# Gathers of two tiles issued as two each, in a DLRM tower kernel

## The chip, the cores and the metric

The kernel runs on one core of a Trainium2 chip. The metric is the device time of an execution in microseconds (us). A core has TensorE (PE in the profile) for matmuls and transposes, VectorE (DVE), ScalarE (ACT), GpSimd (POOL), which here issues the gathers, and SyncE (SP), which issues the plain loads. The engines run side by side and wait for each other through semaphores. Sixteen DMA engines move the data that POOL and SP ask for.

## The reference

A batch of 2048 samples has 32 fields. For each field a table of 1000, 1250 or 12500 rows of 256 floats is looked up with the sample's id. The 32 looked-up rows of a sample are multiplied pairwise, and three dense layers follow:

```
e = stack([tbl_f[ids[:, f]] for f in range(32)], axis=1)      # 2048 x 32 x 256
z = einsum('bnd,bmd->bnm', e, e)[:, iu, ju]                    # the 496 pairs i < j
h = concatenate([z, dense_ctx], axis=1)                        # 496 + 16 = 512 features
h = maximum(h @ W_top1 + b_top1, 0)                            # 512 x 512
h = maximum(h @ W_top2 + b_top2, 0)                            # 512 x 256
y = h @ W_top3                                                 # 256 x 1
```

All is float32.

## The kernel before

The batch is worked in 16 tiles of 128 samples, one sample to a partition. Six of the 32 fields have small tables and are looked up on PE, by matmuls of one-hot columns with a table held on the chip (`look_up`, line 338; VectorE makes the columns, line 674). The other 26 fields are gathered: POOL issues one indirect DMA per field and tile, which fetches for each of the 128 partitions the table row whose number stands in `row_ids` (line 295).

Two fields make a unit, so a tile has 13 units (tile 0 has some more, for 29 gathers); all units of all tiles stand in one list, `UNITS`, which POOL goes through in order. Gathered rows land in `rows`, which has nine places, one unit each. Before unit n is gathered, POOL waits until PE has transposed unit n − 9 (`turn_done`, line 293). Each place has a semaphore, `gathered`, which a gather raises by 16; `n_gathered` says what count PE has to see before it transposes unit n.

PE goes through the tiles in order. For one tile it transposes 13 units into four PSUM banks (`turn`, line 322), from which ScalarE (line 483) and VectorE (line 609) copy them to `turned`; the gram then multiplies the fields of each sample with each other (`gram`, line 358) in eight portions of 64 matmul records, and between the portions stand the lookups of a following tile. Four of the next tile's units are transposed early, after portions 3 to 6, the other nine after the last portion, in `turn_all`. In `turn_all`, too, the features of the tile before are turned, and layer 1 of that tile follows (line 407). ScalarE copies its result out with the bias (line 550), and layer 2 (line 420) runs after portion 0 of the gram. VectorE finishes the tile's output (lines 655 and 657). The last tile has a gram form of its own (line 377) and no lookups.

SP issues the loads in one queue: the row numbers of tile 0, ids and small tables, then the row numbers of tiles 1 to 15 (line 263), more ids, each behind the one-hot that frees its place, the other tables and the weights.

Of the kernel before, what the change touches and what calls it, by code (L numbers as in the profile page):

```python
# [7 lines left out]
FIELDS = 32  # L8
D = 256
P = 128  # L10
# [11 lines left out]
SMALL = len(SMALL_FIELDS)  # L22
SLOTS = SMALL_FIELDS + [f for f in range(FIELDS) if f not in SMALL_FIELDS]
TILES = BATCH // P


def pair_order():

    upper = np.zeros((FIELDS, FIELDS), np.int64)
    rows, cols = np.triu_indices(FIELDS, k=1)  # L30
    upper[rows, cols] = upper[cols, rows] = np.arange(PAIRS)
    upper = upper[np.ix_(SLOTS, SLOTS)]
    order = [upper[i, (i + k) % FIELDS] for i in range(FIELDS) for k in range(1, HALF)]
    order += [upper[i, i + HALF] for i in range(HALF)]
    order += list(range(PAIRS, PAIRS + CONTEXT))
    return np.array(order)


def dlrm_tower(nc, dense_ctx, ids, small_ids, tables, w1, b1, w2, b2, w3, out):
    fp32 = mybir.dt.float32  # L40
    fp32r = mybir.dt.float32r
    int32 = mybir.dt.int32
# [19 lines left out]
    UNITS = [(0, unit) for unit in PAIRED + ODD_PAIRED]  # L62
    BEGIN = [0, len(UNITS)]
# [4 lines left out]
    PLACES = 9  # L68
# [29 lines left out]
    for step in range(-1, TILES):  # L98
        FIRST[step] = len(LOOKUPS)
        n = step + 1  # L100
# [10 lines left out]
    with ctx:  # L111
        def sbuf(name, shape, dt=fp32):
            return ctx.enter_context(nc.sbuf_tensor(name, shape, dt))
# [4 lines left out]
        def sem(name):  # L118
            return ctx.enter_context(nc.semaphore(name))

        row_ids = sbuf("row_ids", [P, TILES, FIELDS], int32)
        ids_across = sbuf("ids_across", [P, IDS_RING, 2 * P], int32)
        row_numbers = sbuf("row_numbers", [SP, SUB], int32)

# [6 lines left out]
        rows = sbuf("rows", [P, PLACES, 2, D])  # L131
# [37 lines left out]
        diagonal = products[:, :].rearrange("p (i k) -> p i k", k=ZROW + 1)  # L169

        row_ids_in = [sem(f"row_ids_in{i}") for i in range(2)]
        ids_across_in = [sem(f"ids_across_in{i}") for i in range(IDS_RING)]
        dense_in = sem("dense_in")
        weights_in = sem("weights_in")
        table_in = [sem(f"table_in{i}") for i in range(SMALL)]
        gathered = [sem(f"gathered{i}") for i in range(PLACES)]
# [49 lines left out]

        def n_gathered(n):

            return 16 * sum(len(UNITS[m][1]) for m in range(n % PLACES, n + 1, PLACES))

        def n_ids(n):

# [4 lines left out]
        @block.sync  # L237
        def _(sp):
            def load_ids(n):
                f, t, tiles = LOOKUPS[n]  # L240
                if n >= IDS_RING:
                    sp.wait_ge(one_hot_made, n - IDS_RING + 1)
                sp.dma_start(ids_across[:, n % IDS_RING, 0:tiles * P],
                             small_ids[f, t * P:(t + tiles) * P].partition_broadcast(P),
                             ).then_inc(ids_across_in[n % IDS_RING], 16)

            def load_table(i):
                table = tables[i].rearrange("(p r) d -> p r d", r=SUB)
                sp.dma_start(landed[0:SP_WIDE, i, :, 1, :], table[0:SP_WIDE, :, :]).then_inc(table_in[i], 16)
                sp.dma_start(landed[SP_WIDE:SP, i, :, 1, :], table[SP_WIDE:SP, :, :]).then_inc(table_in[i], 16)  # L250

            def load_dense(t):
                if t > 0:
                    sp.wait_ge(ft_done, t)
                sp.dma_start(features[:, PAIRS:FEATURES], dense_ctx[t * P:(t + 1) * P, :]).then_inc(dense_in, 16)

            sp.dma_start(row_ids[:, 0, :], ids[:, 0, :]).then_inc(row_ids_in[0], 16)
            load_ids(0)
            load_table(0)
            load_ids(1)  # L260
            load_ids(2)
            load_table(1)
            sp.dma_start(row_ids[:, 1:TILES, :], ids[:, 1:TILES, :]).then_inc(row_ids_in[1], 16)
            load_ids(3)
            load_ids(4)
            for i in range(2, SMALL):
                load_table(i)
            load_dense(0)
            sp.dma_start(w2_sb[:, :, :], w2.rearrange("(k p) n -> p k n", p=P)).then_inc(weights_in, 16)
            sp.dma_start(w3_sb[:, :], w3.rearrange("n a -> (a n)").partition_broadcast(P)).then_inc(weights_in, 16)  # L270
            sp.dma_start(b1_sb[:, :], b1).then_inc(weights_in, 16)
            sp.dma_start(b2_sb[:, :], b2.partition_broadcast(P)).then_inc(weights_in, 16)
            for c in range(KC):
                sp.dma_start(w1_sb[:, c, :], w1[c * P:(c + 1) * P, :]).then_inc(weights_in, 16)
            load_ids(5)
            for t in range(TILES):
                if t + 2 in FIRST:
                    for n in range(FIRST[t + 1], FIRST[t + 2]):
                        load_ids(n)
                if t + 1 < TILES:  # L280
                    load_dense(t + 1)
            sp.wait_ge(y_kept, 1)
            sp.dma_start(out.rearrange("(t p) a -> t (p a)", p=P), y_rows).then_inc(y_out, 16)
            sp.wait_ge(y_out, 16)

        @block.gpsimd
        def _(pool):
            def gather(n):
                t, unit = UNITS[n]
                if n == 0 or n == BEGIN[1]:  # L290
                    pool.wait_ge(row_ids_in[t], 16)
                if n >= PLACES:
                    pool.wait_ge(turn_done, n - PLACES + 1)
                for j, f in enumerate(unit):
                    pool.indirect_dma_start(  # L295
                        out=rows[:, n % PLACES, j, :], out_offset=None, in_=tables[f],
                        in_offset=bass.IndirectOffsetOnAxis(ap=row_ids[:, t, f:f + 1], axis=0),
                    ).then_inc(gathered[n % PLACES], 16)

            pool.memset(ident[:, :], 0.0).then_inc(ident_zero, 1)  # L300
            pool.wait_ge(ident_zero, 1)
            pool.affine_select(out=ident[:, :], in_=ident[:, :], compare_op=ALU.not_equal, fill=1.0,
                               base=0, pattern=[[-1, P]], channel_multiplier=1).then_inc(ident_ready, 1)
            pool.iota(row_numbers[:, :], pattern=[[1, SUB]], base=0,
                      channel_multiplier=SUB).then_inc(row_numbers_ready, 1)
            for n in range(len(UNITS)):
                gather(n)

        @block.tensor
        def _(pe):  # L310
            def turn(n):
                _, unit = UNITS[n]
                pe.wait_ge(gathered[n % PLACES], n_gathered(n))
                if n >= RING:
                    if by_act(n - RING):
                        pe.wait_ge(act_kept, n_act_kept(n - RING))
                    else:
                        pe.wait_ge(dve_kept, n_dve_kept(n - RING))
                for c in range(CHUNKS):
                    for j in range(len(unit)):  # L320
                        at = (c * len(unit) + j) * P
                        last = pe.transpose(turn_ps[n % RING][:, at:at + P],  # L322
                                            rows[:, n % PLACES, j, c * P:(c + 1) * P], ident[:, :])
                last.then_inc(turn_done, 1)

            def look_up(n, first, end):

                f, _, tiles = LOOKUPS[n]
                width = tiles * P
                if first == 0:  # L330
                    pe.wait_ge(one_hot_made, n + 1)
                    if n < SMALL:
                        pe.wait_ge(low_parts, (f + 1) * STEPS)
                    if n > 0:
                        pe.wait_ge(look_kept, n)
                for k in range(first, end):
                    c, r, part = k // (2 * SUB), k // 2 % SUB, k % 2
                    last = pe.matmul(look_ps[:, c * width:(c + 1) * width],  # L338
                                     small[:, f, r, part, c * P:(c + 1) * P], one_hot[n % 2][:, r, 0:width],
                                     start=(r == 0 and part == 0), stop=(r == SUB - 1 and part == 1))  # L340
                if end == PRODUCTS:
                    last.then_inc(looked_up, 1)
# [394 lines left out]
```

## Time and profile before

| what | value |
|---|---|
| time, median of 2 runs | 564.79 us (564.66 to 564.92) |
| span of the profiled execution | 890.7 us (no other time of it is given) |
| PE busy | 601.0 us, 67% |
| PE weight loads busy | 524.1 us, 59% |
| VectorE busy | 225.9 us, 25% |
| ScalarE busy | 204.6 us, 23% |
| POOL busy | 398.0 us, 45%, of which 397.2 us are the 419 gathers |
| DMA | 70.97 MB, mean 80 GB/s |

The profiled execution is much longer than the timed ones, so its shares are not those of a timed run. "Issue" in it is time in which an engine waited for nothing that the profile shows, and "remote" a releaser that it could not find. Durations of POOL's gathers are those of the issuing instruction, not of the data's way.

### The profile page before, as it was taken

The page shows a single profiled execution, that of the slowest core. Times are in us where ns is not written, and L with a number is a line of the kernel's source. Part 1 is how long each engine was busy: PE and PEld are TensorE (multiplying, and loading weights), DVE is VectorE, ACT ScalarE, POOL GpSimd, SP SyncE. Part 2 cuts the span into 40 slices and gives each one's busy share as a digit, 9 for nine tenths or more (in the row PEclk, how much of TensorE's full clock was granted, in tenths as well). Part 3 has the DMA queues.
Part 4 walks back from the last instruction along what each step waited for, and adds up shares of the span by engine and source line. Part 5 has one row for each costly group of instructions (what it writes and reads, how often), then busy time and mean ns, then how long its engine had stood idle before and what let it go on. Part 6 is the DMA issues. An engine that isn't in the chain of part 4 may idle for free.

```text
span 890.7 us, 24184 instructions
## 1 busy us (share of the span) xinstructions
PE 601.0 (67%) x11019; PEld 524.1 (59%) x11019; DVE 225.9 (25%) x578; ACT 204.6 (23%) x369; POOL 398.0 (45%) x426
## 2 busy tenths in 40 slices
PE   3557668486684867748577584875848668486687
PEld 2456557375572756737467474765737657375586
DVE  3444313123130231402223032231312313123122
ACT  4252303103030030401313022130210303103042
POOL 7563625526255361543715347262462625526220
PEclk9688969698796987969789697896969969698799
DMA  9962312313122141321313224131231312313110
GB/s 220 243 204 68 99 42 77 94 44 102 43 78 83 50 107 38 83 73 56 108 37 87 63 57 118 32 96 49 70 105 39 101 41 76 88 41 90 43 38 2
DMA packets 37459, 70.97 MB, mean 80 GB/s; under 512 B 10382, under 2 KB 23438, under 8 KB 37358
## 3 DMA queue, kind: packets, MB, share of 16 engines
q0 software_dynamic: 20112, 54.95, 22.1%
q1 hardware_dynamic: 17246, 14.48, 7.0%
q8 instruction: 87, 1.43, 0.7%
q14 instruction: 14, 0.11, 0.0%
HBM read 69.39 MB, written 0.01 MB: 78 GB/s over the span
## 4 chain that ended last, share of the span: by engine, by line
PE 42%; another core or an unknown queue 30%; issue 13%; ACT 12%; DMA 1%; DVE 1%; POOL 1%; ACTq 0%; DVEq 0%
PE look_ps L338 18%; PE quad_ps L358 12%; PE top_ps L420 6%; ACT turned L501 4%; ACT turned L483 3%; PE turn_ps L322 3%; PE quad_ps L322 2%; ACT area L550 2%; ACT ahead L490 1%; DMA rows<-in_tbl,row_ids 1%; PE quad_ps L377 1%; POOL rows L295 1%; PE top_ps L407 1%; ACT products L506 0%
## 5 line engine op out<-in xcount | busy, mean ns | idle before, releaser
L295 POOL DMA_INDIRECT rows<-in_tbl,row_ids x419 | 397.2, 948 | 458.1 <-PE turn_ps L322 184.1
L338 PE MATMUL look_ps<-one_hot,small 125*128 125x256 f32 (+1 forms) x1536 | 251.9, 303 | 104.7 <-issue 92.8
L338 PEld LDWEIGHTS look_ps<-one_hot,small 125*128 125x128 f32 x1536 | 214.0, 202 | 116.6 <-issue 112.3
L358 PE MATMUL quad_ps<-turned 128*32 128x31 f32 x7680 | 140.0, 204 | 121.8 <-issue 121.5
L358 PEld LDWEIGHTS quad_ps<-turned 128*32 128x32 f32 x7680 | 108.8, 115 | 166.9 <-issue 153.3
L674 DVE TENSOR_SCALAR one_hot<-ids_across,sub_row 125x256 fp32r<-125x256 int32 (+1 forms) x384 | 112.0, 364 | 145.8 <-PE look_ps L338 126.6
L322 PE MATMUL turn_ps<-ident,rows 128*128 128x128 f32 x424 | 64.5, 282 | 28.5 <-issue 14.7
L655 DVE TENSOR_TENSOR top_ps<-top_ps,b_sb 128x256 f32<-128x256 f32 x15 | 6.5, 433 | 299.8 <-PE top_ps L420 299.8
L490 ACT ACTIVATE ahead<-look_ps 128x512 f32<-128x512 f32 (+1 forms) x48 | 28.3, 590 | 232.5 <-PE look_ps L338 219.1
L407 PE MATMUL top_ps<-area,w_sb 128*128 128x128 f32 x488 | 61.9, 276 | 19.5 <-issue 18.8
L550 ACT ACTIVATE area<-top_ps,b_sb 128x128 f32<-128x128 f32 x61 | 17.5, 368 | 227.5 <-remote 225.2
L407 PEld LDWEIGHTS top_ps<-area,w_sb 128*128 128x128 f32 x488 | 57.8, 192 | 18.1 <-issue 17.2
L322 PEld LDWEIGHTS turn_ps<-ident,rows 128*128 128x128 f32 x424 | 48.2, 143 | 31.8 <-issue 28.2
L483 ACT ACTIVATE turned<-turn_ps 128x512 f32<-128x512 f32 x57 | 35.0, 631 | 114.2 <-PE quad_ps L358 76.2
L322 PE MATMUL quad_ps<-ident,rows 128*128 128x128 f32 x414 | 60.1, 279 | 0.8 <-DMA rows<-in_tbl,row_ids 0.8
L483 ACT ACTIVATE turned<-quad_ps 128x512 f32<-128x512 f32 x55 | 33.9, 631 | 90.6 <-PE quad_ps L358 70.8
L420 PE MATMUL top_ps<-w_sb,area 128*128 128x256 f32 x120 | 49.4, 585 | 4.1 <-ACT area L550 4.1
L618 DVE STREAM_TRANSPOSE products<-quad_ps 128x992 f32<-128x992 f32 x15 | 18.3, 1217 | 127.7 <-PE quad_ps L358 127.7
L322 PEld LDWEIGHTS quad_ps<-ident,rows 128*128 128x128 f32 x414 | 46.5, 142 | 2.9 <-DMA rows<-in_tbl,row_ids 1.2
L501 ACT ACTIVATE turned<-ahead 128x768 f32<-128x768 f32 x31 | 45.0, 1552 | 0.0
L420 PEld LDWEIGHTS top_ps<-w_sb,area 128*128 128x128 f32 x120 | 35.6, 311 | 13.9 <-ACT area L550 6.1
L609 DVE COPY turned<-quad_ps 128x512 f32<-128x512 f32 (+1 forms) x49 | 33.0, 681 | 34.1 <-PE quad_ps L322 14.6
(50 smaller groups left out, 169.9 us busy)
## 6 DMA issues: line engine op xcount, KB each, us to landing
rows<-in_tbl,row_ids POOLq DMA_INDIRECT x419
ids_across<-in_small_ids SPq DMA_DIRECT2D x45, 128.0 KB
landed<-in_tbl SPq DMA_DIRECT2D x6, 896.0 KB
w_sb<-in_W_top SPq DMA_DIRECT2D x4, 256.0 KB
landed<-in_tbl SPq DMA_DIRECT2D x6, 104.0 KB
w_sb<-in_W_top SPq DMA_DIRECT2D x1, 512.0 KB
area<-in_dense_ctx SPq DMA_DIRECT2D x16, 8.0 KB
row_ids<-in_ids SPq DMA_DIRECT2D x1, 240.0 KB
```

What stands on the lines that cost most here:

```text
L295: pool.indirect_dma_start(out=rows[:, n % PLACES, j, :], out_offset=None, in_=tables[f], in_offset=bass.IndirectOffsetOnAxis(ap=row_ids[:, ...
L322: last = pe.transpose(turn_ps[n % RING][:, at:at + P], rows[:, n % PLACES, j, c * P:(c + 1) * P], ident[:, :])
L338: last = pe.matmul(look_ps[:, c * width:(c + 1) * width], small[:, f, r, part, c * P:(c + 1) * P], one_hot[n % 2][:, r, 0:width], start=(r ...
L358: last = pe.matmul(gram_ps[q * FIELDS:(q + 1) * FIELDS, g // BANK_GROUPS, at:at + COLS], turned[:, c, s, :], turned[:, c, s, 0:COLS], star ...
L407: last = pe.matmul(bank[:, m * P:(m + 1) * P], w1_sb[:, c, m * P:(m + 1) * P], features_t[:, c, :], start=(c == 0), stop=(c == KC - 1))
L420: last = pe.matmul((last_h2 if t == TILES - 1 else top_ps)[:, 0:HIDDEN2], hidden1[:, c, :], w2_sb[:, c, :], start=(c == 0), stop=(c == M1 ...
L483: act.activation(turned[:, :, :, f:f + len(unit)], turn_ps[n % RING][:, 0:CHUNKS * len(unit) * P].rearrange("p (c f s) -> p c s f", c=CHUN ...
L490: act.activation(ahead[:, f, :, 0:tiles * P], look_ps[:, 0:CHUNKS * tiles * P].rearrange("p (c s) -> p c s", c=CHUNKS), ACT.Copy).then_inc ...
L501: act.activation(turned[:, :, :, fs].rearrange("p c s f -> p f c s"), ahead[:, fs, :, half * P:(half + 1) * P], ACT.Copy).then_inc(placed, 1)
L550: act.activation(hidden1[:, m, :], bank[:, m * P:(m + 1) * P], ACT.Relu, bias=b1_sb[:, m:m + 1]).then_inc(h1_kept, 1)
L609: dve.tensor_copy(turned[:, :, :, f:f + len(unit)], turn_ps[n % RING][:, 0:CHUNKS * len(unit) * P].rearrange("p (c f s) -> p c s f", c=CHU ...
L674: last = dve.tensor_scalar(one_hot[n % 2][:, r, 0:width], ids_across[0:SP, n % IDS_RING, 0:width], sub_row[:, r:r + 1], None, ALU.is_equal)
```

## The change

In tile 4 a gather of 128 rows becomes one of rows 0 to 63 and one of rows 64 to 127; in tile 8, one of rows 0 to 123 and one of rows 124 to 127. Both of a pair raise the semaphore of the unit's place by 16, and the count that PE waits for is doubled for units of these tiles. The row numbers of the second part come from a new array, `row_ids_tail` (64 partitions, 2 × 26 numbers), which the host fills and SP loads once, behind the row numbers of tiles 1 to 15; POOL waits for it ahead of tile 4.

```diff
+SPLIT_AT = {4: 64, 8: 124}
+SPLIT_TILES = sorted(SPLIT_AT)
...
+        row_ids_tail = sbuf("row_ids_tail", [P // 2, len(SPLIT_TILES), FIELDS - SMALL], int32)
...
-            return 16 * sum(len(UNITS[m][1]) for m in range(n % PLACES, n + 1, PLACES))
+            return 16 * sum(len(UNITS[m][1]) * (2 if UNITS[m][0] in SPLIT_AT else 1)
+                            for m in range(n % PLACES, n + 1, PLACES))
...
             sp.dma_start(row_ids[:, 1:TILES, :], ids[:, 1:TILES, :]).then_inc(row_ids_in[1], 16)
+            sp.dma_start(row_ids_tail[:, :, :], tail_ids).then_inc(row_ids_tail_in, 16)
...
+                if t == SPLIT_TILES[0] and n == BEGIN[t]:
+                    pool.wait_ge(row_ids_tail_in, 16)
+                at = SPLIT_AT.get(t, P)
                 for j, f in enumerate(unit):
                     pool.indirect_dma_start(
-                        out=rows[:, n % PLACES, j, :], out_offset=None, in_=tables[f],
-                        in_offset=bass.IndirectOffsetOnAxis(ap=row_ids[:, t, f:f + 1], axis=0),
+                        out=rows[0:at, n % PLACES, j, :], out_offset=None, in_=tables[f],
+                        in_offset=bass.IndirectOffsetOnAxis(ap=row_ids[0:at, t, f:f + 1], axis=0),
                     ).then_inc(gathered[n % PLACES], 16)
+                    if at < P:
+                        tail = row_ids_tail[0:P - at, SPLIT_TILES.index(t), f - SMALL:f - SMALL + 1]
+                        pool.indirect_dma_start(
+                            out=rows[at:P, n % PLACES, j, :], out_offset=None, in_=tables[f],
+                            in_offset=bass.IndirectOffsetOnAxis(ap=tail, axis=0),
+                        ).then_inc(gathered[n % PLACES], 16)
```

## Rows read from the trace of the kernel before

**Rows 1.** The page: its head, busy time by engine, DMA engines' busy tenths in 40 slices.
```profile
span 890.7 us, 24184 instructions
...
PE 601.0 (67%) x11019; PEld 524.1 (59%) x11019; DVE 225.9 (25%) x578; ACT 204.6 (23%) x369; POOL 398.0 (45%) x426
...
DMA  9962312313122141321313224131231312313110
```

**Rows 2.** POOL's gathers: busy us, mean ns, idle before; durations minimum/median/maximum; waits by releaser.
```profile
L295 POOL DMA_INDIRECT rows<-in_tbl,row_ids x419 | 397.2, 948 | 458.1 <-PE turn_ps L322 184.1 <-PE quad_ps L322 164.5 <-issue 101.8
...
L295 POOL DMA_INDIRECT rows<-in_tbl,row_ids x419: 940/946/1098, 2.7 to 855.9; - x140
...
  issue: 101.8, 333
```

**Rows 3.** Timeline of POOL in one tile: start, duration, instruction, idle before, releaser.
```profile
351.74 0.94 POOL L295 DMA_INDIRECT rows<-in_tbl,row_ids  x1 [15.15 <-PE turn_ps L322]
...
369.02 0.94 POOL L295 DMA_INDIRECT rows<-in_tbl,row_ids  x1 [3.12 <-PE turn_ps L322]
...
390.25 0.95 POOL L295 DMA_INDIRECT rows<-in_tbl,row_ids  x1 [0.30 <-issue]
```

**Rows 4.** Timeline of PE and ACT in the same tile.
```profile
341.08 3.40 PE L420 MATMUL top_ps<-w_sb,area 128*128 128x256 f32 x8 [0.27 <-ACT area L550]
344.13 1.66 PE L338 MATMUL look_ps<-one_hot,small 125*128 125x256 f32 x11
345.72 0.76 PE L358 MATMUL quad_ps<-turned 128*32 128x31 f32 x64
...
352.71 0.59 PE L358 MATMUL quad_ps<-turned 128*32 128x31 f32 x42
...
354.80 0.66 PE L322 MATMUL turn_ps<-ident,rows 128*128 128x128 f32 x4
...
375.80 0.83 PE L407 MATMUL top_ps<-area,w_sb 128*128 128x128 f32 x6
...
380.39 0.28 PE L338 MATMUL look_ps<-one_hot,small 125*128 125x256 f32 x1 [0.42 <-issue]
...
394.56 1.14 ACT L550 ACTIVATE area<-top_ps,b_sb 128x128 f32<-128x128 f32 x4 [16.39 <-remote]
395.75 0.79 PE L420 MATMUL top_ps<-w_sb,area 128*128 128x256 f32 x1 [0.27 <-ACT area L550]
```

**Rows 5.** Timeline of PE and ACT in the last tile, the same step.
```profile
863.80 3.74 PE L407 MATMUL top_ps<-area,w_sb 128*128 128x128 f32 x32
...
867.58 1.14 ACT L550 ACTIVATE area<-top_ps,b_sb 128x128 f32<-128x128 f32 x4 [0.95 <-PE top_ps L407]
868.77 1.99 PE L420 MATMUL top_ps<-w_sb,area 128*128 128x256 f32 x8 [0.15 <-ACT area L550]
```

**Rows 6.** Two windows: length, busy (count) by engine; then granted clock, DMA share, GB/s.
```profile
341.08:344.10 3.02, 3.02 (x8) 2.46 (x8) 0.00 (x0) 0.00 (x0) 0.00 (x0) 0.52 0.02 5
868.77:870.70 1.93, 1.93 (x9) 1.44 (x9) 0.00 (x0) 0.00 (x0) 0.00 (x0) 1.00 0.00 0
```

**Rows 7.** Timeline of POOL: the first and the last gather.
```profile
2.71 1.10 POOL L295 DMA_INDIRECT rows<-in_tbl,row_ids  x1 [1.15 <-DMA row_ids<-in_ids]
...
855.87 0.95 POOL L295 DMA_INDIRECT rows<-in_tbl,row_ids  x1 [0.31 <-issue]
```

**Rows 8.** Timeline of POOL: its first wait for a place.
```profile
37.57 0.95 POOL L295 DMA_INDIRECT rows<-in_tbl,row_ids  x1 [5.00 <-remote]
```

**Rows 9.** The gathers' DMA queue (packets, MB, share of 16 engines); the iota on POOL.
```profile
q0 software_dynamic: 20112, 54.95, 22.1%
...
L304 POOL IOTA row_numbers<- 125x8 int32 x1 | 0.1, 125 | 0.0
```

**Rows 10.** Timeline of SP's queue around the load of the row numbers.
```profile
6.03 1.11 SPq L263 DMA_DIRECT2D row_ids<-in_ids  x1
7.24 6.32 SPq L243 DMA_DIRECT2D ids_across<-in_small_ids  x2
```

More of the change, by code:

```diff
@@ L36, in pair_order, with dlrm_tower @@
     return np.array(order)
-def dlrm_tower(nc, dense_ctx, ids, small_ids, tables, w1, b1, w2, b2, w3, out):
+def dlrm_tower(nc, dense_ctx, ids, tail_ids, small_ids, tables, w1, b1, w2, b2, w3, out):
     fp32 = mybir.dt.float32
@@ L171, in dlrm_tower @@
         row_ids_in = [sem(f"row_ids_in{i}") for i in range(2)]
+        row_ids_tail_in = sem("row_ids_tail_in")
         ids_across_in = [sem(f"ids_across_in{i}") for i in range(IDS_RING)]
@@ L726 @@
     laid["ids"] = np.ascontiguousarray(by_slot.reshape(TILES, P, FIELDS).transpose(1, 0, 2))
+    tails = np.zeros((P // 2, len(SPLIT_TILES), FIELDS - SMALL), np.int32)
+    for k, t in enumerate(SPLIT_TILES):
+        tails[:P - SPLIT_AT[t], k] = laid["ids"][SPLIT_AT[t]:, t, SMALL:]
+    laid["tail_ids"] = tails
     laid["b_top1"] = np.ascontiguousarray(laid["b_top1"].reshape(-1, P).T)
@@ L732 @@
     out = nc.dram_tensor("out_y", (BATCH, 1), mybir.dt.float32, kind="ExternalOutput").ap()
-    dlrm_tower(nc, aps["dense_ctx"], aps["ids"], aps["small_ids"], [aps[f"tbl_{f}"] for f in SLOTS],
+    dlrm_tower(nc, aps["dense_ctx"], aps["ids"], aps["tail_ids"], aps["small_ids"], [aps[f"tbl_{f}"] for f in SLOTS],
                aps["W_top1"], aps["b_top1"], aps["W_top2"], aps["b_top2"], aps["W_top3"], out)
```

## The prediction

> **What bounds the kernel now.** The page's head comes first. The profiled execution spans 890.7 us [rows 1]; no other time of its own is given. The timed runs have a median of 564.79 us, 326 us less, so any share read from this trace belongs to a slower execution, and the first question is which engine was slowed. By busy share GpSimd (POOL) at 45% looks harmless beside TensorE (PE) at 67% [rows 1].
>
> The groups by line and the waits say what POOL does: 419 gathers of 0.948 us, 0.306 us of "issue" after another (101.8 us in 333 times), and 349 us of waiting for PE's transposes to free a place [rows 2]. Its timeline in one tile shows a long wait of 15.15 us, and later a gather every 1.25 us (369.02 to 390.25 in 17 steps) [rows 3]. So a tile's 26 gathers need 26 × 1.25 = 32.5 us, and POOL has 22.2 us free in the profiled period of 54.67 us (layer 2 starts at 341.08 and 395.75) [rows 4].
>
> Now PE in that period. A portion of 64 gram matmuls takes 0.76 us, 11 lookups take 1.66 us. After 376.6 the same kinds of instruction start one per 0.7 us or slower (0.28 us long, 0.42 us idle before), and what ends the idle time is "issue", nothing that the profile shows; ScalarE waits 16.39 us for layer 1 beside it [rows 4]. In the last tile the same step has no such stretch: after layer 1 (32 matmuls, 3.74 us) ScalarE has waited 0.95 us, and layer 2 starts at 868.77 [rows 5]. I therefore take the slow stretch out. From 376.6 to layer 2 at 395.75 there are 19.1 us for work that takes about 2.6 us dense (11 lookups, 64 gram, two of layer 1), so 16.5 us go; four gram portions with a transpose or the tile's end behind them took about 2.1 us instead of 0.7 (one from 352.71 to 354.80), so some 5.7 us go. 54.67 − 16.5 − 5.7 leaves 32.4 us. Layer 2 there ran at a granted clock of 0.52, near the lower of the two levels (1.2 GHz), and took 3.02 us to its last start against 1.93 us at 1.00 (2.4 GHz) in the last tile [rows 6]. So PE needs 31 to 32.4 us, against POOL's 32.5 us.
>
> The sum of POOL alone settles which it is. First gather at 2.71 us, 418 steps of 1.25 us, 0.95 us for the last: it would end at 526 us if POOL never waited. From the end of the last gather (855.87 + 0.95 = 856.8) to the end of the span are 33.9 us [rows 7]. Together that is 560 us, against 564.79 us timed. So in the timed runs POOL's waits come to some 5 us in all, a few more if the tail is shorter there, and the trace has one of 5.00 us already in the first tile [rows 8]. Behind it POOL hardly waits: **its queue of gathers sets the pace.**
>
> **The change, part by part.** In tiles 4 and 8 each of the 26 gathers becomes two: 52 more, 471 in all. Rows moved, places, transposes and all work of PE, ScalarE and VectorE stay as they are.
>
> *The gathers.* Take a gather as a part F that does not depend on its rows, and a part that does, with 0.30 us between two. Splitting repeats F and the 0.30 us, wherever the cut lies: both tiles pay 26 × (0.30 + F), the even and the uneven one. The trace has gathers of 128 rows alone, so F is bounded only: at F = 0 the sum is 52 × 0.30 = 15.6 us, at F = 0.95 us it is 52 × 1.25 = 65 us. Which end is nearer? The gathers last 0.940 to 1.098 us with a median of 0.946 [rows 2], and one at 37.57 us, while the DMA engines are over 90% busy, takes the same 0.95 us as one at 390.25 [rows 1, 3, 8]: the time does not follow the moving of data. Half a gather is nearest to a whole one, and 124 rows are almost one; for 4 rows the only other nearby row is a POOL instruction of 0.125 us [rows 9], which is not a DMA. I take F at four fifths, 0.76 us, a choice and not a reading: 52 × 1.06 = 55 us. The Trainium skill, "DMA: Bandwidth & Descriptors", section "Anatomy of one DMA — SWDGE (gpsimd) path", calls descriptor generation small and says that many descriptors can be emitted before the incremental cost shows; by that F is nearly all, and the sum would be 65 us. No row here has a second size to test it.
>
> *What hides it.* At most POOL's own waits, 5 us over the run and mostly before tile 4; I deduct 1 us. Places stop POOL no more than before: while it works on a split tile, PE stands at the transposes and frees each place as its unit lands.
>
> *Who waits behind it.* PE's transposes of the units of tiles 4 and 8, then the evacuations, the gram, and layer 1 of the tile before, all in order. The following tiles run at POOL's pace, so nothing is given back. PE will idle some 27 us in each split tile and may come back at the lower clock, as in the tile's window [rows 6]; its margin of up to 1.5 us a tile and POOL's lead cover most of that, so it is 0 to 3 us, taken as 0.
>
> *The extra load* of the tail's row numbers is one DMA more on SP's queue, behind the one that ends at 7.14 us. Its neighbours take some 1 us to issue. Behind it stand loads of ids and tables; the next, with 6.32 us for two transfers, waits for a one-hot in between [rows 10], and that wait hides it. Without the cover it costs 1 us. POOL's new wait for it falls at tile 4, long after.
>
> Sum: 564.8 + 55 − 1 = **619 us**.
>
> In the profiled execution itself the same work shows less. A split tile needs 32.5 + 27.6 = 60 us of POOL in a period of 54.67 us: with every wait filled 5 us stick out, with only the long one of 15.15 us filled 12 us, twice. So its span goes from 890.7 us up by 11 to 25 us.
>
> **Rivals.**
>
> *The fixed part is nearly all* (F = 0.95 us): 630 us. For it speaks the steadiness of the gathers' durations; against it, that 128 rows must cost something. Chance 0.3.
>
> *The cost goes mostly by rows* (F up to 0.38 us): 15.6 to 35 us, so 580 to 600 us. The gap of 0.30 us remains even at F = 0, so this is still slower. Chance 0.12.
>
> *Few DMA engines for 124 rows.* The gathers' queue took 22.1% of 16 engines' 890.7 us [rows 9], 7.5 engine-us a gather, 0.47 us on each of 16. If 124 rows, which do not divide by 16, go over four engines, each is busy 1.8 us, and a unit lands 1.4 us later. Once, that adds 1.4 us. If it were always the same four, tile 8 would need 26 × 1.9 = 49 us of them, below POOL's 60 us; they become the bound only from 1.23 times that time per row on, and at 1.5 times the result is some 632 us, with more beyond. Chance 0.06. The Trainium skill, same page, section "Why a DMA increments its semaphore by 16 and not by 1", has such a rule: the engine count is the largest number up to 16 that divides the slowest dimension. By it 124 and 4 rows get four engines each, and 64 rows 16.
>
> *POOL is not the bound (not slower).* Suppose that the timed runs are the profiled one shrunk as a whole, gathers too, by 564.8/890.7. Then POOL is free 14 us in a period of 34.7 us, and a tile's extra work is 26 × 1.06 × 0.63 = 17.5 us: 3.5 us stick out of each tile, 572 us. It hides wholly from F = 0.55 us down, and the time stays at 565 us. Against it: the gathers' 1.25 us are the same where PE is dense and where it crawls, and the slow stretches are PE's alone. Chance 0.06.
>
> **How the numbers follow.** The forecast's own case (F from 0.38 to 0.9 us, 600 to 627 us) has the remaining 0.46. With the fixed end, 0.3, and the upper third of the row-proportional case, the range from 594 to 635 us holds some 0.8. A measurement of this kernel can tell 2%, 11.3 us, from no change. Slower by more than that: all cases but the last, with its few outcomes beyond 576 us: 0.93. Within 2%: 0.06. Faster by 2%: 0.01; nothing is taken off POOL's queue.
>
> **What would show it.** 471 gathers, those of tiles 4 and 8 in pairs, with 0.30 us between two; the durations of the forms with 64 and 4 rows give F at once, about 0.85 and 0.77 us by my choice. In tiles 4 and 8, POOL at its "issue" pace without a long wait, and PE idle before transposes, released by the gathers' DMA. Both tiles longer by the same amount; if tile 8 is longer than tile 4, it is the DMA engines or the uneven count. Wrong at the root would be a long wait of POOL for PE inside a split tile of a run that is no slower than before.

## The result, and the profile after

The changed kernel takes 634.62 us (634.57 to 634.66) against 564.79 us: 69.8 us more. The two medians give a ratio of 1.124; over the fast runs it is 1.126 (95% interval 1.120 to 1.132). The forecast was slower by 54 us, to 619 us, so the direction and the place were right and the size was not.

The page after, answering to [rows 1] and [rows 2]: span, busy time by engine, granted clock by slice, the gathers' DMA queue, the chain's shares, and the gathers' two lines (L305 the first parts and all whole gathers, L311 the second parts).

```profile
span 632.8 us, 24238 instructions
...
PE 522.7 (83%) x11019; PEld 478.4 (76%) x11019; DVE 231.2 (37%) x578; ACT 204.1 (32%) x369; POOL 453.2 (72%) x478
...
PEclk9987999999955999999995559999999989999988
...
q0 software_dynamic: 23856, 54.99, 31.1%
...
POOL rows L305 22%; PE look_ps L354 19%; PE quad_ps L374 10%; POOL rows L311 7%; PE top_ps L423 7%; DMA rows<-in_tbl,row_ids 5%; PE quad_ps L338 4%; PE turn_ps L338 4%; PE top_ps L436 3%; ACT turned L499 1%; PE quad_ps L393 1%; DMA rows<-in_tbl,row_ids_tail 1%; PE top_ps L413 1%; ACT area L528 1%; ACT ahead L506 1%
...
L305 POOL DMA_INDIRECT rows<-in_tbl,row_ids x419 | 405.5, 968 | 130.5 <-issue 118.0
...
L311 POOL DMA_INDIRECT rows<-in_tbl,row_ids_tail x52 | 46.9, 901 | 15.8 <-issue 15.8
```

This profiled execution spans 632.8 us, close to its timed runs; it lacks the slow stretches of PE that made the one before 890.7 us long. So the two spans are not compared, only durations and waits. POOL is busy 72% of the time, and its 471 gathers with 0.30 us behind each fill nearly all of the span up to 600 us: of its idle time 134 us are "issue". Before, 349 us were waits for a place; now there are 11 (us in total, times, longest):

```profile
POOL rows L305 <- PE quad_ps L338: 7.1, 17, 2.0
...
POOL rows L305 <- PE turn_ps L338: 4.3, 14, 0.3
```

POOL's timeline at both ends of tile 4 and of tile 8:

```profile
139.17 0.91 POOL L305 DMA_INDIRECT rows<-in_tbl,row_ids  x1 [0.31 <-issue]
140.39 0.91 POOL L311 DMA_INDIRECT rows<-in_tbl,row_ids_tail  x1 [0.30 <-issue]
...
201.98 0.96 POOL L305 DMA_INDIRECT rows<-in_tbl,row_ids  x1 [0.30 <-issue]
...
299.73 1.30 POOL L305 DMA_INDIRECT rows<-in_tbl,row_ids  x1 [0.30 <-PE turn_ps L338]
301.34 0.90 POOL L311 DMA_INDIRECT rows<-in_tbl,row_ids_tail  x1 [0.30 <-issue]
...
371.06 0.99 POOL L311 DMA_INDIRECT rows<-in_tbl,row_ids_tail  x1 [0.30 <-issue]
372.35 0.96 POOL L305 DMA_INDIRECT rows<-in_tbl,row_ids  x1 [0.31 <-issue]
```

Tile 4 takes POOL 201.98 − 139.17 = 62.8 us, tile 8 takes 372.35 − 299.73 = 72.6 us, where 26 whole gathers take 26 × 1.25 = 32.5 us. The two differences, 30.3 and 40.1 us, add up to 70.4 us: the whole of the measured 69.8 us. And the tiles are not alike.

Durations of the four forms (minimum/median/maximum in ns; first the 64 and 64 rows of tile 4, then the 124 and 4 rows of tile 8, with two whole gathers at the start of that window):

```profile
L305 POOL DMA_INDIRECT rows<-in_tbl,row_ids x26: 894/898/925, 139.2 to 199.6; - x26
...
L311 POOL DMA_INDIRECT rows<-in_tbl,row_ids_tail x26: 902/907/908, 140.4 to 200.8; - x26
...
L305 POOL DMA_INDIRECT rows<-in_tbl,row_ids x28: 949/1284/1337, 297.2 to 369.5; - x28
...
L311 POOL DMA_INDIRECT rows<-in_tbl,row_ids_tail x26: 885/892/989, 301.3 to 371.1; - x26
```

The surprise is the third: a gather of 124 rows lasts 1.28 us, longer than one of 128 rows (0.946 us), while 4 rows last as long as 64.

PE in tile 8, its waits for the second parts over the run, and the granted clock of both split tiles (windows: length, busy time of PE, PEld, DVE, ACT, POOL, then clock, DMA share, GB/s):

```profile
PE turn_ps L338 <- DMA rows<-in_tbl,row_ids_tail: 32.6, 8, 4.7
PE quad_ps L338 <- DMA rows<-in_tbl,row_ids_tail: 30.2, 9, 4.7
...
357.61 1.11 PE L338 MATMUL quad_ps<-ident,rows 128*128 128x128 f32 x4 [4.38 <-DMA rows<-in_tbl,row_ids_tail]
...
139.17:201.98 62.81, 37.21 (x724) 32.48 (x722) 16.94 (x44) 15.66 (x26) 46.97 (x52) 0.77 0.25 66
300.00:372.35 72.35, 37.38 (x713) 31.79 (x711) 16.81 (x43) 14.77 (x25) 56.51 (x52) 0.73 0.24 57
```

PE stands 63 us at transposes whose second part has not landed, 17 times, and its granted clock falls to 0.5 within each split tile (the PEclk row above), the lower of the two levels. That adds nothing that the runs show: in the tile behind, layer 2 follows layer 2 after 30.86 us (382.04 to 412.90), less than POOL's 32.5 us.

```profile
382.04 1.99 PE L436 MATMUL top_ps<-w_sb,area 128*128 128x256 f32 x8
...
412.90 2.00 PE L436 MATMUL top_ps<-w_sb,area 128*128 128x256 f32 x8
```

### The profile page after: what moved, and what is told of

It is laid out like the page before. It is cut to its first block, busy times and chain, and to the rows that moved or that the text cites. A ratio compares the mean times of both kernels' runs of the same rounds, so it can differ in the third digit from the quotient of the medians.

```text
span 632.8 us, 24238 instructions
## 1 busy us (share of the span) xinstructions
PE 522.7 (83%) x11019; PEld 478.4 (76%) x11019; DVE 231.2 (37%) x578; ACT 204.1 (32%) x369; POOL 453.2 (72%) x478
## 2 busy tenths in 40 slices
DMA packets 41285, 71.03 MB, mean 112 GB/s; under 512 B 14103, under 2 KB 27263, under 8 KB 41183
## 3 DMA queue, kind: packets, MB, share of 16 engines
q0 software_dynamic: 23856, 54.99, 31.1%
## 4 chain that ended last, share of the span: by engine, by line
PE 49%; POOL 29%; issue 11%; DMA 6%; ACT 4%; DVE 2%; POOLq 0%; ACTq 0%; DVEq 0%
POOL rows L305 22%; PE look_ps L354 19%; PE quad_ps L374 10%; POOL rows L311 7%; PE top_ps L423 7%; DMA rows<-in_tbl,row_ids 5%; PE quad_ps L338 4%; PE turn_ps L338 4%; PE top_ps L436 3%; ACT turned L499 1%; PE quad_ps L393 1%; DMA rows<-in_tbl,row_ids_tail 1%; PE top_ps L413 1%; ACT area L528 1%; ACT ahead L506 1%
## 5 line engine op out<-in xcount | busy, mean ns | idle before, releaser
L305 POOL DMA_INDIRECT rows<-in_tbl,row_ids x419 | 405.5, 968 | 130.5 <-issue 118.0
L354 PE MATMUL look_ps<-one_hot,small 125*128 125x256 f32 (+1 forms) x1536 | 222.1, 294 | 7.3 <-DVE small L680 6.6
L354 PEld LDWEIGHTS look_ps<-one_hot,small 125*128 125x128 f32 x1536 | 196.5, 194 | 10.8 <-issue 8.5
L690 DVE TENSOR_SCALAR one_hot<-ids_across,sub_row 125x256 fp32r<-125x256 int32 (+1 forms) x384 | 117.4, 377 | 116.3 <-PE look_ps L354 110.4
L374 PE MATMUL quad_ps<-turned 128*32 128x31 f32 x7680 | 103.4, 199 | 0.4 <-issue 0.3
L374 PEld LDWEIGHTS quad_ps<-turned 128*32 128x32 f32 x7680 | 85.8, 110 | 20.3 <-issue 0.6
L338 PE MATMUL quad_ps<-ident,rows 128*128 128x128 f32 x414 | 65.1, 291 | 37.6 <-DMA rows<-in_tbl,row_ids_tail 30.2
L423 PE MATMUL top_ps<-area,w_sb 128*128 128x128 f32 x488 | 62.8, 291 | 0.7 <-ACT area L552 0.7
L499 ACT ACTIVATE turned<-quad_ps 128x512 f32<-128x512 f32 x55 | 33.9, 632 | 80.1 <-PE quad_ps L374 40.6
L311 POOL DMA_INDIRECT rows<-in_tbl,row_ids_tail x52 | 46.9, 901 | 15.8 <-issue 15.8
L625 DVE COPY turned<-turn_ps 128x512 f32<-128x512 f32 x49 | 33.3, 690 | 54.5 <-PE turn_ps L338 54.4
L436 PE MATMUL top_ps<-w_sb,area 128*128 128x256 f32 x120 | 29.9, 392 | 0.2 <-ACT area L566 0.2
```

What stands on the lines that cost most here:

```text
L305: pool.indirect_dma_start(out=rows[0:at, n % PLACES, j, :], out_offset=None, in_=tables[f], in_offset=bass.IndirectOffsetOnAxis(ap=row_ids ...
L311: pool.indirect_dma_start(out=rows[at:P, n % PLACES, j, :], out_offset=None, in_=tables[f], in_offset=bass.IndirectOffsetOnAxis(ap=tail, a ...
L338: last = pe.transpose(turn_ps[n % RING][:, at:at + P], rows[:, n % PLACES, j, c * P:(c + 1) * P], ident[:, :])
L354: last = pe.matmul(look_ps[:, c * width:(c + 1) * width], small[:, f, r, part, c * P:(c + 1) * P], one_hot[n % 2][:, r, 0:width], start=(r ...
L374: last = pe.matmul(gram_ps[q * FIELDS:(q + 1) * FIELDS, g // BANK_GROUPS, at:at + COLS], turned[:, c, s, :], turned[:, c, s, 0:COLS], star ...
L423: last = pe.matmul(bank[:, m * P:(m + 1) * P], w1_sb[:, c, m * P:(m + 1) * P], features_t[:, c, :], start=(c == 0), stop=(c == KC - 1))
```

## The experiments

**One tile alone.** `SPLIT_AT = {4: 64}` in the first run, `{8: 124}` in the second.

```diff
-SPLIT_AT = {4: 64, 8: 124}
+SPLIT_AT = {4: 64}          # or {8: 124}
```

> Only tile 4 is split, into 64 and 64 rows; tile 8 is as before. Theory (the gathers' queue on GpSimd never waits, so each tile adds its own gather time): 26 x (2 x 1.206 - 1.253) = 30.1 us, so 594.9 us. Rival (most of the price belongs to the second of two split tiles, because TensorE and the clock have not recovered from the first): clearly under 30 us, some 585 us.

> Only tile 8 is split, into 124 and 4 rows. Theory: 26 x (1.28 + 0.89 + 0.60 - 1.25) = 39.6 us, so 604.4 us, and the 124-row gathers last 1.28 us again. Rival (the longer gathers come from the state that the split of tile 4 leaves behind): they last 0.95 us, 30.9 us more, 595.7 us.

Measured beside 562.36 us before: 593.47 us, ratio 1.053 (1.047 to 1.060), 31 us more; and 603.32 us, ratio 1.074 (1.067 to 1.081), 41 us more. Each tile pays its own share, and the 124-row gathers of the second run are as long as beside the other split (the first row again with one whole gather in its window):

```profile
L305 POOL DMA_INDIRECT rows<-in_tbl,row_ids x27: 944/1281/1339, 269.1 to 340.0; - x27
...
L311 POOL DMA_INDIRECT rows<-in_tbl,row_ids_tail x26: 884/888/958, 271.9 to 341.6; - x26
```

The rival of a state left behind by tile 4 falls.

**Another cut of tile 8.**

```diff
-SPLIT_AT = {4: 64, 8: 124}
+SPLIT_AT = {4: 64, 8: 112}
```

> Tile 4 into 64 and 64 rows, tile 8 into 112 and 16 instead of 124 and 4. Theory (a gather's time follows the largest number of rows that one DMA engine gets; 112 and 16 divide by 16, so 7 rows and 1 row): 112 rows last about 0.94 us, 16 rows 0.89 us; tile 8 adds 30.6 us, 625.5 us in all. Rival (a long part beside a short one is dear whatever the counts): 112 rows last about 1.25 us, 634 us.

Measured: 621.57 us, ratio 1.105 (1.097 to 1.112), 59 us more than before and so 28 us for tile 8, where the durations below give 26 × (0.922 + 0.852 + 2 × 0.30 − 1.25) = 29 us. The 112 and the 16 rows:

```profile
L305 POOL DMA_INDIRECT rows<-in_tbl,row_ids x26: 918/922/976, 300.9 to 360.5; - x26
...
L311 POOL DMA_INDIRECT rows<-in_tbl,row_ids_tail x26: 847/852/856, 302.1 to 361.8; - x26
```

A long part beside a short one is not dear in itself; 124 rows are. The forecast's linear picture holds among counts that divide by 16: 16 rows 0.852, 64 rows 0.90, 112 rows 0.922, 128 rows 0.946 us.

**Ten cuts in one kernel.**

```diff
-SPLIT_AT = {4: 64, 8: 124}
+SPLIT_AT = {3: 89, 4: 126, 5: 125, 6: 122, 7: 120, 8: 112, 9: 96, 10: 93, 11: 62, 12: 31}
...
-                        tail = row_ids_tail[0:P - at, SPLIT_TILES.index(t), f - SMALL:f - SMALL + 1]
+                        tail = row_ids[0:P - at, t, f:f + 1]
```

> Ten tiles with ten cuts; the second part of a gather takes the row numbers of the first rows again, so the output is not the reference's. Theory (the time follows the rows on one engine, when the engine count is the largest number up to 16 that divides the rows; 16, 64, 112 and 128 rows gave 0.836 us + 0.0137 us for each row on one of 16 engines, 4 and 124 rows some 0.03 us more): 126 rows (9 on each of 14) 0.99, 125 (25) 1.21, 122 (61) 1.70, 120 (8) 0.97, 112 (7) 0.93, 96 (6) 0.92, 93 and 62 and 31 (31 each) 1.28, 89 (89) 2.08, 97 (97) 2.19, 66 (6) 0.95 us. Rival one (any count that is no multiple of 16 pays one flat price): 126, 125, 122, 120, 93, 89, 62 and 66 rows all 1.28 us. Rival two (the price is for fewer engines, not for rows on one): 31 rows last longer than 62, 62 longer than 93, 93 longer than 124.

Measured: 989.0 us in one run, from which only durations are read (first parts L305, second parts L311, by the tile's window):

```profile
L305 POOL DMA_INDIRECT rows<-in_tbl,row_ids x25: 974/974/1187, 205.3 to 264.9; - x25
...
L305 POOL DMA_INDIRECT rows<-in_tbl,row_ids x25: 1181/1187/1668, 270.3 to 334.9; - x25
...
L305 POOL DMA_INDIRECT rows<-in_tbl,row_ids x25: 1675/1682/1697, 338.0 to 414.1; - x25
...
L305 POOL DMA_INDIRECT rows<-in_tbl,row_ids x24: 987/989/997, 422.2 to 479.7; - x24
...
L305 POOL DMA_INDIRECT rows<-in_tbl,row_ids x25: 1276/1282/1292, 612.2 to 680.1; - x25
...
L305 POOL DMA_INDIRECT rows<-in_tbl,row_ids x26: 1275/1280/1284, 682.9 to 753.7; - x26
L311 POOL DMA_INDIRECT rows<-in_tbl,row_ids x25: 933/937/1036, 684.5 to 752.4; - x25
...
L305 POOL DMA_INDIRECT rows<-in_tbl,row_ids x25: 1254/1258/1272, 757.8 to 854.1; - x25
L311 POOL DMA_INDIRECT rows<-in_tbl,row_ids x26: 2139/2146/2155, 755.3 to 855.7; - x26
...
L305 POOL DMA_INDIRECT rows<-in_tbl,row_ids x26: 2046/2050/2060, 107.6 to 196.8; - x26
```

In their order: 126, 125, 122, 120, 93, 62 and 66, 31 and 97, 89 rows. Set beside the rule that the engine count is the largest number up to 16 that divides the rows:

| rows | engines by the rule | rows on one | expected us | measured us |
|---|---|---|---|---|
| 66 | 11 | 6 | 0.95 | 0.937 |
| 120 | 15 | 8 | 0.97 | 0.989 |
| 126 | 14 | 9 | 0.99 | 0.974 |
| 125 | 5 | 25 | 1.21 | 1.187 |
| 124 (changed kernel) | 4 | 31 | | 1.284 |
| 93 | 3 | 31 | 1.28 | 1.282 |
| 62 | 2 | 31 | 1.28 | 1.280 |
| 31 | 1 | 31 | 1.28 | 1.258 |
| 122 | 2 | 61 | 1.70 | 1.682 |
| 89 | 1 | 89 | 2.08 | 2.050 |
| 97 | 1 | 97 | 2.19 | 2.146 |

Both rivals fall: 126 and 120 rows, which do not divide by 16, pay next to nothing, and 31 rows on one engine last as long as 93 on three. A 97-row gather costs POOL more than twice a 128-row one.

**Fewer gathers.** The kernel before, with one of the 26 gathers left out in each of tiles 1 to 15, or four (`LEFT_OUT` is a list of units whose second field isn't fetched).

```diff
+LEFT_OUT = [8]              # or [2, 5, 8, 11]
...
-                for j, f in enumerate(unit):
+                for j, f in enumerate(fetched(n)):
```

> The kernel before, without one of the 26 gathers in each of tiles 1 to 15 (its place keeps older rows, so the output is not the reference's; all of TensorE's work stays). Theory (GpSimd's gathers set the pace, TensorE needs 30.9 us a tile by a tile of the changed kernel in which it did not wait): 15 x 1.253 = 18.8 us less than before. Rival (GpSimd has slack, TensorE or the chain through it sets the pace): 0 to 3 us less.

> As before with four gathers left out in each of tiles 1 to 15. Theory: GpSimd needs 27.5 us a tile, TensorE 30.9 us, so TensorE becomes the bound: 15 x (32.6 - 30.9) = 25 us less than before, not 75 us, and GpSimd waits for places in every tile. Rival one (GpSimd is the bound with much room under it): 60 x 1.253 = 75 us less. Rival two (TensorE is the bound already): no change.

Measured beside 565.11 us before: 544.32 us, ratio 0.963 (0.960 to 0.966), 21 us less; and 545.55 us, ratio 0.966 (0.962 to 0.969), 20 us less. POOL's waits in the first, then in the second (us in total, times, longest):

```profile
POOL rows L300 <- PE quad_ps L327: 8.0, 12, 4.3
POOL rows L300 <- PE turn_ps L327: 2.7, 9, 0.3
```

```profile
POOL rows L300 <- PE quad_ps L327: 43.0, 47, 6.6
POOL rows L300 <- PE turn_ps L327: 38.1, 43, 1.8
```

The first gather taken off a tile is worth its full 1.25 us (18.8 us expected); the next three only make POOL wait, 81 us in place of 11. So POOL was the bound before, with TensorE 1.3 us a tile behind it (20 us in 15 tiles). The expected 25 us for the second run were 5 us too many: TensorE needs 31.2 us a tile rather than 30.9. The second run's profile shows the same directly, with layer 2 every 31.1 to 31.3 us except at the end (at 272.29 and 303.44 us, for one).

**Added gathers under a cover.** Four gathers left out as above, and two of the others split in each of tiles 1 to 15.

```diff
+                    at = P // 2 if j == 0 and halved(n) else P
+                    for k in range(P // at):
...
+                            out=rows[k * at:(k + 1) * at, n % PLACES, j, :], out_offset=None, in_=tables[f],
+                            in_offset=bass.IndirectOffsetOnAxis(ap=row_ids[0:at, t, f:f + 1], axis=0),
```

> As in the run with four gathers left out a tile, and two of the 22 that remain go out as 64 and 64 rows in each of tiles 1 to 15, so 30 instructions more (second parts take the row numbers of the first rows again; the output is not the reference's). Theory (an added gather costs only where GpSimd has no time free; here a tile needs 27.5 + 2 x 1.16 = 29.9 us of it and TensorE 30.9 us): the same as without the splits, some 20 us less than the kernel before. Rival (an added gather costs its time wherever it stands, for instance through later landing): 30 x 1.16 = 34.8 us more than without the splits, 15 us more than the kernel before.

Measured: 549.86 us beside 564.20 us before, ratio 0.973 (0.968 to 0.979). Without the splits the ratio was 0.966 (0.962 to 0.969). So some 4 us are left of the 34.8 us, with intervals that overlap a little; the rest is hidden where POOL has time free. POOL's waits say so:

```profile
POOL rows L307 <- PE quad_ps L334: 28.1, 28, 7.4
POOL rows L307 <- PE turn_ps L334: 18.1, 21, 1.8
```

They fell from 81 to 46 us, by 35 us, the time of the 30 added gathers. The 4 us, if they are more than scatter, stand on PE: in the two profiles (runs of 545.9 and 553.9 us) its gram matmuls were busy 99.2 us without the splits and 106.0 us with them. What slows them is not shown.

**The load alone.** The changed kernel with `at = P` throughout, so without a split, and the count that PE waits for as before.

```diff
-            return 16 * sum(len(UNITS[m][1]) * (2 if UNITS[m][0] in SPLIT_AT else 1)
+            return 16 * sum(len(UNITS[m][1])
...
-                at = SPLIT_AT.get(t, P)
+                at = P
```

> The changed kernel with its extra array and its load on SyncE's queue, but no gather split. Theory (the load is hidden behind a wait of the queue): within 1 us of the kernel before, GpSimd's gathers 0.95 us as before. Rival (the load delays the ids or the tables of the first tile, or the shifted buffers change something): some us more.

Measured: 563.75 us beside 564.20 us, ratio 0.999 (0.997 to 1.001). The load costs nothing that the runs can tell (under 2 us by the interval). Its profile shows the unsplit kernel without slow stretches: span 559.7 us, POOL waiting for places 12.9 us in all, the longest wait 2.8 us.

```profile
span 559.7 us, 24186 instructions
...
POOL rows L305 <- PE quad_ps L338: 8.0, 17, 2.8
POOL rows L305 <- PE turn_ps L338: 4.9, 16, 0.3
```

## Why the prediction was right in place and wrong in size

*The bound.* Right, and shown. The sum of POOL alone, 526 us to the last gather's end against 33.9 us of tail, had left some 5 us of waits. In the unsplit profile the 33 waits of 12.9 us include the usual 0.30 us between two gathers, about 10 us; that leaves 3 us. Its tail is 29 us (the last gather starts at 529.5 us), so the 33.9 us of the slow profile were some 5 us too many. Leaving out one gather a tile gave its full time back.

*PE's slow stretch as a thing of that one profile.* Right: 31 to 32.4 us a tile was the estimate, and the runs with fewer gathers put it at 31.2 us. The forecast for the profiled span (11 to 25 us more) fell, since the next profile had no such stretch; on the timed runs nothing hung on it.

*The gathers, tile 4.* The form of the term, 26 × (0.30 + F), was right, and F was taken too small: 0.86 us (0.898 + 0.907 − 0.946, two halves against a whole) instead of 0.76 us, so the tile cost 30.3 us and not 27.6. The rule that many descriptors can be emitted before the cost shows (the Trainium skill, "DMA: Bandwidth & Descriptors", section "Anatomy of one DMA — SWDGE (gpsimd) path") was nearer: from 16 to 128 rows a gather grows from 0.852 to 0.946 us.

*The gathers, tile 8.* This step failed: "Splitting repeats F and the 0.30 us, wherever the cut lies". The cut decides, since the part that depends on rows follows the rows on the most loaded DMA engine and not all rows. 124 rows pay 0.34 us more than 128, 26 times: 8.8 us. With F too small again, and some 0.03 us more for the 4 rows, the tile cost 40 us instead of 27.6 us. The bound of 65 us was no bound, because it let a gather of fewer rows be at most as long as a whole one, and 70 us came out. That 634.62 us still lies at the upper edge of the stated 594 to 635 us is luck: the prediction let both tiles grow by the same amount there.

*The rival of few DMA engines.* It had the right rule (the Trainium skill, same page, section "Why a DMA increments its semaphore by 16 and not by 1"; the ten forecast counts of rows agree with it to 0.05 us, and so do the packets in the last section) and the wrong price. It was priced where the data moves, 1.4 us of landing once, and asked whether DMA engines become the bound. They did not: POOL's own instruction is what gets longer.

*Waiters and cover.* Right: PE idles, loses its clock, and has it back before it counts; measured and summed differ by 0.6 us, too little to tell the 1 us deducted as cover from none. The load: right, 0 within the noise.

## What to carry to other kernels

Where gathers set the pace, count instructions first: 16 rows cost nine tenths of 128, and each instruction brings 0.30 us besides. If a gather must be cut, cut at a multiple of 16, as measured here for rows of 1 KB: 112 and 16 rows cost 2.38 us a pair, 124 and 4 rows 2.78 us. And before trusting shares of a profile that is much longer than the timed runs, add up the queue that has a fixed pace and see whether it fills the timed run by itself.

## What the runs showed of the hardware

An indirect gather's time on GpSimd was about 0.84 us + 0.0135 us for each row on the DMA engine with the most rows, where the rows divide by 16, and up to 0.04 us more where fewer engines have rows, up to 97 rows on one (2.146 us).

The packets of the gathers' queue in three windows of the changed kernel (tile 4, tile 8, a stretch of whole gathers):

```profile
q0 software_dynamic: 1573, 3.23, 21.1%
```

```profile
q0 software_dynamic: 4562, 3.48, 20.8%
```

```profile
q0 software_dynamic: 3839, 10.49, 36.4%
```

A whole gather makes 3839 / 80 = 48 packets, a pair of 64 and 64 rows 1573 / 25 = 63, a pair of 124 and 4 rows 4562 / 26 = 175, for the same data. Nearly all of the added ones are under 512 B (14103 in the run after, 10382 before).

One count gives them all: for each of 16 engines one closing packet, and one for every four rows (4096 B), rounded up, of the engine with the most rows. That is 16 × 3 = 48, twice 16 × 2 = 64, and 16 × 9 + 16 × 2 = 176. With the engine counts of the rule it gives 23856 packets for the whole changed kernel and 63792 for the ten cuts, and the pages have just these:

```profile
q0 software_dynamic: 63792, 55.52, 22.8%
```

So the engines without rows are sent as many packets as the loaded ones. The sizes in the changed kernel's trace say what these hold: it has 2184 packets of 16 B and 312 of 12 B, where the kernel before has none. For each 124-row gather that is 84 and 12, or 31 pieces of 4 B for each of twelve engines: a filler for each of the 31 rows that each of the other four has. That GpSimd's time goes into making the fillers would fit, with 0.0135 us for 16 pieces. No run here took the fillers away, so this last step stays a reading; that GpSimd waits for the loaded engines instead was not ruled out.
